# Weight loads put into TensorE's order behind VectorE's steps, and LN4's statistics as one stream, in an eight-core two-layer kernel

## What is computed

```python
# x: (8, 2048, 1024), each core one row of the batch
x = x + L0_attn(layernorm(x))   # LN1; log-space gated scan over tokens (Wz, Wh), layernorm of h, + input
x = x + L0_ffn(layernorm(x))    # LN2; W_fc (4096x1024) and W_proj (1024x4096), both fake-quantised to
                                # 8 bits by max|W|, plus a rank-16 term each; gelu between them
x = x + L1_attn(layernorm(x))   # LN3; time mix, k, v, r = three 1024x1024 products, WKV recurrence over
                                # tokens, sigmoid(r) * wkv, then Wo (1024x1024)
x = x + L1_ffn(layernorm(x))    # LN4; three 1024x1024 products in a row, tanh
```

## Time and profile before

| | us |
|---|---|
| median of the timed runs (2) | 2946.6 (2922.14 and 2971.07) |
| the profiled execution, its own time | 2919.07 |
| its span on the slowest core (core 5) | 2917.5 |
| spans of the eight cores | 2888.3 to 2917.5 |
| granted TensorE clock, mean of each core | 0.703 to 0.729 of full speed |

### The profile page before, as it was taken

The page is one execution under the profiler, slowest core; times in us unless marked ns, Lnnn a source line. Parts: engine busy times, 40 slices in busy tenths (PEclk is TensorE's granted clock), DMA queues, the critical chain, the costliest instruction groups (busy, mean ns, idle before and its releaser), DMA issues.

```text
span 2917.5 us, 18494 instructions; the slowest of 8 cores (2888.3 to 2917.5 us)
## 1 busy us (share of the span) xinstructions
PE 1361.3 (47%) x4868; PEld 487.2 (17%) x4868; DVE 1505.5 (52%) x1759; ACT 592.8 (20%) x689; POOL 278.6 (10%) x219
## 2 busy tenths in 40 slices
PE   3144444004044804978888531265055554413884
PEld 0011110000000300333333200022022211101331
DVE  3866667888898997101010137655754414144321
ACT  0023330000187400040303000044125300000023
POOL 0300000120310001000000002500310001022000
PEclk9997775555555955989999855588578655656998
DMA  7223331340033330101010571100100042464025
GB/s 188 87 86 116 109 105 32 79 123 15 17 106 112 102 108 13 37 22 51 8 58 1 96 161 57 43 0 0 36 7 0 13 107 50 103 103 122 0 78 146
DMA packets 73843, 196.76 MB, mean 67 GB/s; under 512 B 9440, under 2 KB 9440, under 8 KB 70928
## 3 DMA queue, kind: packets, MB, share of 16 engines
q1 hardware_dynamic: 57648, 157.37, 18.7%
q0 software_dynamic: 14080, 23.53, 5.6%
q10 hardware_dynamic: 2016, 14.68, 1.4%
HBM read 179.24 MB, written 39.85 MB: 75 GB/s over the span
## 4 chain that ended last, share of the span: by engine, by line
DVE 38%; PE 23%; DMA 19%; ACT 9%; issue 8%; POOL 2%; DVEq 1%; SPq 1%; ACTq 0%; POOLq 0%
PE PB L38 23%; DVE SC L38 9%; DVE X L38 9%; DVE E L38 6%; DMA SC<-SP 5%; DVE AT L38 5%; ACT L38 4%; DVE XB L38 4%; DMA AT<-SP 3%; DVE H L38 3%; DMA XB<-SP 3%; DMA E<-WPRT 2%; DMA E<-SP 2%; ACT X L38 2%; DVE MX L38 2%
## 5 line engine op out<-in xcount | busy, mean ns | idle before, releaser
L38 ACT ACT_TABLE_LOAD x218 | 279.7, 1283 | 2308.7 <-PE PB L38 966.4
L38 PE MATMUL PB<-XB,X 128*128 128x512 bf16 x1280 | 298.6, 393 | 134.9 <-POOL XB L38 59.2
L38 PE MATMUL PB<-XB,H 128*128 128x512 bf16 x896 | 239.7, 428 | 254.2 <-DVE X L38 149.6
L38 PE MATMUL PB<-E,H 128*128 128x512 bf16 x1152 | 275.8, 404 | 51.5 <-DVE X L38 32.1
L38 PE MATMUL PB<-X,H 128*128 128x512 bf16 x512 | 147.0, 459 | 321.5 <-ACT SC L38 114.9
L38 DVE TENSOR_SCALAR AT<-PB,QS,SMT 128x512 f32<-128x512 f32 x32 | 25.9, 810 | 465.0 <-PE PB L38 335.1
L38 PE MATMUL PB<-SC,ONESB 128*128 128x512 bf16 x256 | 129.5, 609 | 163.6 <-DVE SC L38 140.6
L38 PEld LDWEIGHTS PB<-XB,X 128*128 128x128 bf16 x1280 | 125.6, 100 | 308.0 <-issue 176.4
L38 PEld LDWEIGHTS PB<-XB,H 128*128 128x128 bf16 x896 | 92.3, 107 | 402.0 <-issue 336.3
L38 PEld LDWEIGHTS PB<-E,H 128*128 128x128 bf16 x1152 | 117.6, 103 | 209.7 <-issue 91.6
L38 PE MATMUL PB<-H,X 128*128 128x512 bf16 x512 | 124.1, 399 | 38.8 <-ACT X L38 29.6
(11 more groups left out here) (148 smaller groups left out, 1942.1 us busy)
## 6 DMA issues: line engine op xcount, KB each, us to landing
AT<-WFCT SPq DMA_DIRECT2D x32, 512.0 KB, 3.5
E<-WFCT SPq DMA_DIRECT2D x32, 512.0 KB, 3.8
SC<-WPRT SPq DMA_DIRECT2D x32, 512.0 KB, 3.7
SC<-SP SPq DMA_DIRECT2D x64, 256.0 KB, 3.4
E<-SP SPq DMA_DIRECT2D x56, 256.0 KB, 5.1
AT<-SP SPq DMA_DIRECT2D x24, 512.0 KB, 3.6
E<-SP SPq DMA_DIRECT2D x24, 512.0 KB, 3.7
X<-XT SPq DMA_DIRECT2D x2, 4096.0 KB, 28.6
```

Of the source, the lines that this page charges most:

```text
L38: ins = f(*args, **kw)
```

## The change

A function `warm()` is added. It appends to PE's order a wait for DVE's latest mark at that point of the program, and two weight loads of ONESB (no matmul). It is called 182 times: after each of the 32 pieces of the combine loop, after each of 6 pieces into which `xh2_v` is cut, after each of the 64 chunks of the two `pass2`, after each of the 16 blends, three times in each of the 16 rounds of the WKV loop (after `ev1b`, `v1` and `v2`), and after each of the 16 steps of `xh4`.

LN4's statistics are moved behind all of WO as one `ln_stream_stats` over both halves, with `stage="sg"`: loads of 128x1024 f32 on SP's queue into three buffers, and for each of 32 tiles of 512 tokens a copy to bf16 on ACT, a square on POOL and two matmuls that accumulate over the 8 blocks. `_ln_rows` then makes mean and factor for all 2048 tokens. The loads of fw1, fa1 and fa2 now stand ahead of this stream on POOL's queue, and the copy `l4cp` is gone.

```diff
@@ -260,6 +260,16 @@
             for i in idxs:
                 if banks[i] is not None:
                     ctx.wait(*banks[i])
+
+        WRHS = bc16(_ap(XB0))[:, 0:512]
+
+        def warm():
+            at = {"vector": k.ch["vector"].val}
+            k.dep(["tensor"], at=at)
+            def wf(t):
+                t.ldweights(ONESB[:])
+                t.ldweights(ONESB[:])
+            k.T(wf)
 
         def gdma(wn, out, in_, gate=None, **kw):
             c = k.ch["gd_" + wn]
@@ -741,6 +751,7 @@
                 if m < 6:
                     xring.release(ci, comb_done[(m, n)])
                     ci += 1
+                warm()
         comb_m = {m: tmax(*(comb_done[(m, n)] for n in range(NT)))
                   for m in range(8)}
 
@@ -758,9 +769,9 @@
         ln2_rows = ln_stats(lambda kk, n: Hr[kk][:, n * NSZ:(n + 1) * NSZ],
                             lambda kk, n: comb_done[(kk, n)], EX[0], EX[1])
         xh2_tok = {}
-        k.dep(["vector", "gpsimd"], at=tmax(ln2_rows))
-        def xh2_v(v):
-            for kk in (0, 1, 2, 4, 5, 6):
+        for kk in (0, 1, 2, 4, 5, 6):
+            k.dep(["vector"], at=tmax(ln2_rows) if kk == 0 else None)
+            def xh2_v(v, kk=kk):
                 for n in range(NT):
                     sl = slice(n * NSZ, (n + 1) * NSZ)
                     v.tensor_sub(SCR[2][:], Hr[kk][:, sl], EX[0][:, sl])
@@ -768,7 +779,9 @@
                     v.tensor_mul(XBF[kk][:, sl], SCR[2][:], EX[1][:, sl])
                     v.chain()
                 xh2_tok[kk] = ("vector", k.ch["vector"].val)
-        k.V(xh2_v)
+            k.V(xh2_v)
+            warm()
+        k.dep(["gpsimd"], at=tmax(ln2_rows))
         def xh2_g(g):
             for kk in (3, 7):
                 for n in range(NT):
@@ -1254,102 +1271,11 @@
                     g1_done[(th, m)] = tok
                     rw_done[(th, m)] = tok
                 k.V(v2)
+                warm()
 
         mloop_v = ("vector", k.snap("vector"))
         mloop_s = ("scalar", k.snap("scalar"))
         mloop_g = ("gpsimd", k.snap("gpsimd"))
-
-        XBF32 = _ap(XB0).bitcast(F32)
-        l4slot = [bc16(_ap(XB0))[:, 8192:10240],
-                  bc16(_ap(XB0))[:, 10240:12288]]
-        l4acc = [XBF32[:, 6144:7168], XBF32[:, 7168:8192]]
-        l4bk = [0]
-        ln4_fin = {}
-        ln4_hidden = {}
-
-        def ln4_need_th(h2):
-            return ((h2 + 1) * CH - 1) // TH
-
-        def ln4_gate(kk, h2):
-            toks = []
-            for j in range(CH // 512):
-                pos = h2 * CH + j * 512
-                toks.append(sp1_done[(kk, pos // TH, (pos % TH) // 512)])
-            return tmax(*toks)
-
-        def emit_ln4_half(h2, free_tok, fin_gate):
-            hidden = ln4_hidden[h2]
-            accX = l4acc[0] if hidden else EX[0][:, h2 * CH:(h2 + 1) * CH]
-            accX2 = l4acc[1] if hidden else EX[1][:, h2 * CH:(h2 + 1) * CH]
-            toks = [free_tok, free_tok]
...
-        for h2 in range(NCH):
-            ln4_hidden[h2] = (ln4_need_th(h2) == 0 and NCH == 2)
 
         x2ring = Ring(k, [SCR[i][:, 0:512] for i in range(4)],
                       ["rr0", "rr1", "rr2", "rr3"], issue_eng="sync",
@@ -1403,16 +1329,8 @@
                     ri2 += 1
             if th == 0:
                 wo_th0 = ("tensor", k.snap("tensor"))
-                for h2 in range(NCH):
-                    if ln4_hidden[h2]:
-                        emit_ln4_half(h2, wo_th0, None)
 
         phaseC_T = ("tensor", k.snap("tensor"))
-        l4free = tmax(phaseC_T, ("gpsimd", k.snap("gpsimd")),
-                      *(ln4_fin[h] for h in range(NCH) if ln4_hidden[h]))
-        for h2 in range(NCH):
-            if not ln4_hidden[h2]:
-                emit_ln4_half(h2, l4free, None)
 
         gdma("fw1", w8_out(Xf[0]), w8_in(FW1, 0), gate=[phaseC_T])
         gdma("fw1", w8_out(Xf[1]), w8_in(FW1, 1))
@@ -1436,19 +1354,23 @@
 
         qring.free = [phaseC_T, phaseC_T]
 
-        at = tmax(mloop_v, *(ln4_fin[h] for h in range(NCH)))
-        k.dep(["vector"], at=at)
-        def l4cp(v):
-            for h2 in range(NCH):
-                if ln4_hidden[h2]:
-                    v.tensor_copy(EX[0][:, h2 * CH:(h2 + 1) * CH], l4acc[0])
-                    v.chain()
-                    v.tensor_copy(EX[1][:, h2 * CH:(h2 + 1) * CH], l4acc[1])
-                    v.chain()
-            v.memset(MX[:, 15:16], 0.0)
-            v.mark()
-        k.V(l4cp)
-        ln4_rows = ("vector", k.snap("vector"))
+        def ln4_gate(kk, h2):
+            toks = []
+            for j in range(CH // 512):
+                pos = h2 * CH + j * 512
+                toks.append(sp1_done[(kk, pos // TH, (pos % TH) // 512)])
+            return tmax(*toks)
+
+        XBF32 = _ap(XB0).bitcast(F32)
+        ln4ring = Ring(k, [XBF32[:, 4096:5120], XBF32[:, 5120:6144],
+                           XBF32[:, 6144:7168]],
+                       ["l40", "l41", "l42"], issue_eng="sync",
+                       free=[wo_th0, wo_th0, wo_th0])
+        ln4_rows = ln_stream_stats(
+            lambda kk: SP1[kk * 128:(kk + 1) * 128, :],
+            ln4_gate, EX[0], EX[1], ln4ring, stage="sg",
+            stage_free=(wo_th0, wo_th0),
+            tiles=(XBF32[:, 7168:7680], XBF32[:, 7680:8192]))
 
         xh4_tok = {}
         li4 = 0
```

More of the change, by code:

```diff
@@ L1280, in emit_ln4_half @@
-        def emit_ln4_half(h2, free_tok, fin_gate):
-            hidden = ln4_hidden[h2]
-            accX = l4acc[0] if hidden else EX[0][:, h2 * CH:(h2 + 1) * CH]
-            accX2 = l4acc[1] if hidden else EX[1][:, h2 * CH:(h2 + 1) * CH]
-            toks = [free_tok, free_tok]
[L1285 to L1331, removed]
-                v.chain()
-                v.tensor_scalar(accX2, accX2, 1.0 / D, LN_EPS,
-                                OP.mult, OP.add)
-                v.chain()
-                v.tensor_mul(tmp, accX, accX)
-                v.chain()
-                v.tensor_sub(accX2, accX2, tmp)
-                v.chain()
-                v.reciprocal(accX2, accX2)
-                v.mark()
-            k.V(l4f)
-            k.dep(["scalar"], ["vector"])
-            def l4s(s, accX2=accX2):
-                s.activation(accX2, accX2, AF.Sqrt)
-                s.mark()
-            ln4_fin[h2] = None
-            k.S(l4s)
-            ln4_fin[h2] = ("scalar", k.snap("scalar"))
```

## The result

The changed kernel is slower: 3169.98 us (median of 11 runs, 3164.49 to 3229.11) against 2930.45 us (median of 10 runs of the kernel before), ratio 1.0829 with a 95% interval of 1.0806 to 1.0851. The medians are 240 us apart; the ratio stands for 242. The forecast was 3153 in a range of 3105 to 3210. (Medians here hold all runs; ratios leave out those in which one die, four of the eight cores, ran over 1% longer at a lower clock, or which lay over 1.5% above the fastest of their kernel.)

What follows compares the result with a forecast made beforehand. No engine is full and the chain changes hands, so a wait costs only where engines now overlap. Terms 67 + 157 + 5 + 5 = 234 on 2919 gave 3153 us, range 3105 to 3210.

Steps and rivals of the forecast that it cites:

- pass2: Feed-forward: waits of the second matrix hold the first tile's mfc until DVE ends; +67 us (60 to 75).
- WKV loop: m loop: mkv(m+1) starts only after v2(m), so its overlap with DVE is lost; +157 us (+139 to +184).
- WO's start: First half's mwo now follows the last v2, and its 16 matmuls precede the first addition; +5 us (0 to 6).
- WO and LN4 up to the first `xh4`: WO runs through, slow loads beside weights' traffic, then 32 stream tiles and the row step; +6.5 us.
- behind it: After xh4's start: loads free of weights' traffic take 9 us off, mm1 no longer under xh4 adds 7.
- The reading of PE's order: PE takes instructions in order, so a waiting warm() holds what follows, as mfc starting at 953.34 suggested.
- The upper bound (35): WKV loop: at most 35 us a round, 8 x 35 = 280 us a half, +184 us in all.
- Rival 1: Loads keep PE at 2.4 GHz, mkv takes 7.1 us instead of 9.1; 35 us less, 3118 us; chance 0.12.
- Rival 2: PE stays at 1.2 GHz in the WKV loop; +112 us, 3265 us; chance 0.05.
- Rival 3: A waiting weight load doesn't hold matmuls behind it; LN4 alone decides, 2924 us, at best 2893; chance 0.04.
- Rivals 4 and 5: 4: one overlap survives, 2996 or 3086 us, chance 0.06; 5: more contention or longer fc merge, about 3205, chance 0.09.
- LN4: Statistics moved behind WO: shorter WO against slow loads and a longer exposed stream; together +5 us (-26 to +25).

Runs made afterwards that it cites:

- the run with late weights: Kernel without any warm() (LN4 moved), loads of fw1, fa1, fa2 put behind LN4's statistics on POOL's queue: 2904.31 us, 0.9909 to the kernel before.

## Why the prediction was right, point by point

The terms, each as forecast and as the stage table has it: `pass2` 67 and 66.9; WKV loop 157 and 167.4; WO's start 5 and 5.3; WO and LN4 up to the first `xh4` +6.5 and +7.6; behind it -2 and -2.0; sum 234 and 245. (The stages that the sum leaves alone add -1, so that the table has 244.)

- **The reading of PE's order.** Start of `mfc`, 63 us of idle DVE, fc merges under the second `pass2`, `mkv` behind `v2`: each is in the trace where it was said to be. Runs with only the waits and with only the loads show that it is the wait.
- **The mis-sized term** is the WKV round. As mean of the cores, seven periods of a half take 34.15 us each and the last round 33.0, where 33.5 and 32.2 were forecast: 272 us against 266.7. The step from `v2` to `mkv` was 0.9 and is 0.94. Most of the rest is `mkv`: I averaged toward 9.0 us, since two rows of m = 0 had 8.63 and 8.77 and the later ones up to 9.6. After 20 us of idle it took 9.4 to 9.75 in 92 of 128 rounds, 9.5 in the mean. Half a microsecond in 14 rounds and 0.8 in two is 8 to 9 of the missing 10 us. The upper bound (35) held it.
- **Rival 1 (the loads keep PE at 2.4 GHz)** had a chance of 0.12 and was wrong: 2, 40 or 100 loads leave the halves at 272 us. The Trainium skill (TensorE: Matmul & The Clock Gate, "What's actually happening") ties the clock to how busy PE has been; in these runs matmuls did raise it and weight loads alone did not, so its rule holds here for matmuls.
- **Rival 2 (PE stays at 1.2 GHz)** was wrong: the later matmuls of each `mkv` and all of `mr` (3.61 us) are at 2.4 GHz, as the granted clock of 1.00 in 1985 to 1998 shows. **Rival 3 (the wait holds nothing behind it)** was wrong; the costs in `pass2`, in the WKV loop and at WO's start are such holds. **Rivals 4 and 5** didn't come: both overlaps were lost in full, and the fc merges ended 28 us ahead of the end of `pass2` (29 forecast).
- **LN4** came out right to 1 us, but by errors that cancel in part, which is luck. The prediction also has the statistics' second half follow the last addition before; its first load was in fact issued 19 us ahead of it, which the sum doesn't use. WO and the stream's loads lost 16 + 4 to the traffic, where I took 23 + 8. Against that WO's pace without traffic was slower than the 5.15 us taken: in the run with late weights 166.7 / 31 = 5.4. The tile pace of 2.05 and the row step were as read. Behind the first `xh4` the 9 us came (-9.3 without `warm()`), though only about half of them is shown to be the weights' traffic, and `warm()` took 7.3 back.
- **The base.** The sum was made on one execution of 2919. The median before is 2930 over ten runs, 11 us above it. That is 11 of the 17 us from 3153 to 3170; the other 6 are the difference itself, 240 between the medians (244 in the table) against 234.

## What to carry to other kernels

A wait put in an in-order engine's queue must be read against everything behind it in program order: price it by the overlap that the trace shows there, and find the cost of one round without overlap in the trace itself (here the first round of each loop). A filler that is to keep an engine's clock up must not wait for another engine's last result, and must be work that raises the clock. Before rearranging a stage, see which queue paces it: moving 32 stores off the queue that issues the loads gave 2.3% here. The rearranged statistics stage gave nothing by itself, 0.9% with the weights behind it, and with the stores moved as well 4.5%.

## What the runs showed of the hardware that was not expected

- Weight loads of 128x128 bf16 stand with 0.10 us each in the trace, but back to back 100 take 4.73 us, 0.047 each. 102 in a row right ahead of `mkv` left it at 9.52 us; 11 matmuls of 512 columns made it 7.07 in 85 of 128 rounds.
- Two runs of matmuls need no slow start if PE isn't stopped between them: WO's groups took 4.9 to 6.4 us each behind a stop, and take 3.61 each in a row of thirteen, with 0.4 us between them.
- ACT loads its table ahead of each of the stream's 32 copies, though they are all the same: 1.28 us of 2.05.
